# Router logits taken as eight extra columns of two projections, in a pre-LayerNorm linear-attention and mixture-of-experts kernel

## What is computed

```python
scores = jnp.einsum('bhld,bhsd->bhls', Q, K)
out = jnp.einsum('bhls,bhsd->bhld', scores * causal, V)   # then @ wo.T + wo_b
x = x + attention(layernorm(x))
xm = layernorm(x).reshape(-1, 128)
logits = xm @ Wg                     # 128 x 8
probs = softmax(logits); topk_p, topk_i = top_k(probs, 2)
# for each token and each of its 2 experts e, weighted with topk_p:
h = relu(xm @ W1[e] + b1[e]); ye = h @ W2[e] + b2[e]
x = x + weighted sum of the two ye
```

## Time and profile before

| | us |
|---|---|
| median of 3 runs | 308.91 (308.56 to 309.41) |
| the profiled execution | 308.35 |
| its span (first to last instruction) | 306.6 |

### The profile page before, as it was taken

How to read it: one execution, slowest core, us unless ns; L and a number is a source line. 1 busy time by engine, 2 the same in 40 slices (tenths; PEclk the granted TensorE clock), 3 DMA queues, 4 the chain that set the end, 5 groups by cost and what they waited for, 6 DMA issues and landing times.

```text
span 306.6 us, 6357 instructions
## 1 busy us (share of the span) xinstructions
PE 244.9 (80%) x1392; PEld 176.5 (58%) x1392; DVE 195.5 (64%) x584; ACT 174.1 (57%) x701; POOL 179.1 (58%) x175
## 2 busy tenths in 40 slices
PE   0589999999999999987779976969399999896000
PEld 0234566666666666655557865857388778774000
DVE  5938999889998989999652456323143343342184
ACT  3243358888888888777678743445155556552000
POOL 3255492205868686876361777777777676676100
PEclk9999999999999999999566998899689999999655
DMA  7940000000111110111160222234443333211499
GB/s 208 310 145 0 1 2 0 0 4 17 37 37 35 38 36 28 43 36 55 34 169 17 62 74 66 70 84 127 132 116 103 92 89 87 68 47 36 155 356 310
DMA packets 32400, 25.50 MB, mean 83 GB/s; under 512 B 4305, under 2 KB 30169, under 8 KB 32364
## 3 DMA queue, kind: packets, MB, share of 16 engines
q1 hardware_dynamic: 23808, 14.52, 17.6%
q0 software_dynamic: 4320, 8.47, 8.4%
q10 hardware_dynamic: 4236, 2.10, 2.3%
HBM read 13.92 MB, written 11.61 MB: 83 GB/s over the span
## 4 chain that ended last, share of the span: by engine, by line
PE 53%; issue 13%; DVE 10%; DMA 9%; POOL 5%; ACT 4%; SPq 3%; ACTq 1%; POOLq 0%; DVEq 0%
PE ps L870 17%; PE ps L840 8%; PE ps L967 6%; PE ps L956 6%; POOL returned L402 4%; DMA back<-returned 3%; PE ps L879 2%; DMA returned<-y_sb,xt 2%; PE ps L892 2%; PE ps L842 2%; SPq L321 2%; DVE back L623 2%; POOL dispatched L374 2%; DVE o_sb L636 2%; PE ps L861 2%
## 5 line engine op out<-in xcount | busy, mean ns | idle before, releaser
L402 POOL DMA_INDIRECT returned<-y_sb,xt x71 | 70.4, 991 | 34.2 <-issue 20.9
L374 POOL DMA_INDIRECT dispatched<-rows,slot x64 | 64.3, 1005 | 37.8 <-ACT rows L473 21.5
L793 DVE TENSOR_SCALAR y_sb<-ps,xt 128x128 f32<-128x128 f32 x71 | 24.9, 350 | 73.4 <-PE ps L968 72.4
L870 PE MATMUL ps<-back,causal 128*128 128x512 f32 x128 | 62.8, 614 | 0.4 <-DVE back L614 0.4
L967 PE MATMUL ps<-w_sb,hT 128*128 x284 | 52.1, 309 | 6.4 <-DVE y_sb L793 4.8
L956 PE MATMUL ps<-xT,w_of 128*128 128x128 f32 x284 | 50.0, 302 | 2.7 <-ACT hT L546 1.9
L538 ACT ACTIVATE xT<-ps 128x128 f32<-128x128 f32 x71 | 19.6, 276 | 55.6 <-PE ps L949 54.4
L967 PEld LDWEIGHTS ps<-w_sb,hT 128*128 128x128 f32 x284 | 40.1, 204 | 19.0 <-issue 18.8
L358 POOL TENSOR_TENSOR back<-qkv 128x1024 f32<-128x1024 f32 x16 | 31.3, 1955 | 31.4 <-ACT qkv L494 31.1
L546 ACT ACTIVATE hT<-ps,b_col 128x128 f32<-128x128 f32 x142 | 43.9, 364 | 1.7 <-PE ps L956 1.4
L956 PEld LDWEIGHTS ps<-xT,w_of 128*128 128x128 f32 x284 | 40.0, 204 | 5.0 <-issue 4.1
(11 more groups left out here) (142 smaller groups left out, 415.9 us busy)
## 6 DMA issues: line engine op xcount, KB each, us to landing
xt<-dispatched SPq DMA_DIRECT2D x71, 65.0 KB, 2.0
back<-returned SPq DMA_DIRECT2D x8, 512.0 KB, 7.6
x_sb<-x SPq DMA_DIRECT2D x8, 256.0 KB, 5.0
out<-x_sb ACTq DMA_DIRECT2D x8, 256.0 KB, 6.6
returned<-y_sb,xt POOLq DMA_INDIRECT x71, 2.3
w_sb<-w SPq DMA_DIRECT2D x1, 1024.0 KB, 5.9
w_sb<-w SPq DMA_DIRECT2D x2, 512.0 KB, 7.2
dispatched<-rows,slot POOLq DMA_INDIRECT x64, 2.4
```

The lines of the kernel that those rows point to most:

```text
L374: pool.indirect_dma_start(out=dispatched[:, :], out_offset=bass.IndirectOffsetOnAxis(ap=slot[:, g * K + k:g * K + k + 1], axis=0), in_=row ...
L402: pool.indirect_dma_start(out=returned[:, :], out_offset=bass.IndirectOffsetOnAxis(ap=xt[:, n % G, D:D + 1].bitcast(I32), axis=0), in_=y_s ...
L793: dve.tensor_scalar(y_sb[:, n % G, :], ps_y, xt[:, n % G, D + 1:D + 2], None, ALU.mult).then_inc(y_done, 1)
L870: mm = pe.matmul(ps_run[g % 2][:, u, :], causal[:, :], outer[:, g % OUTER_RING, 512 * u:512 * (u + 1)], start=True, stop=True)
```

## The change

The logits are no longer computed from the transposed, normalized second tile. Wg is centred once (each column minus its mean), so that the mean of a token drops out of the product, and it then stands as 8 columns beside the weights of two projections: behind Wq, Wk, Wv (`wqkv_sb` has 392 columns), and behind Wo as Wo times the centred Wg (`wo_sb` has 136), with its part of the bias. ScalarE writes the 8 columns of the first projection, times the first LayerNorm's deviation, beside x in `x_sb` (tiles of 136 columns now); VectorE's residual addition is 136 wide and its last 8 columns are the logits, but for the second reciprocal deviation, with which `softmax_start` multiplies them. The stages `gate`, `transpose2` and `xn2T_out` are gone. Softmax, top two, places and rank run one slot earlier, `chosen` one slot earlier and ahead of `rows_out` in ScalarE's slot, and the dispatches lag 15 slots. The first count is waited for 3 slots earlier, and the first table is built in VectorE's slot 30 and no longer 32. GpSimd makes the outer products of all tiles but 13, 16, 19, 22, 25, 28 and 31, which VectorE makes. The block steps still begin at slot 36.

```diff
-    STATE_AFTER = 7
+    STATE_AFTER = 6
+    DISPATCH = 15
+    FIRST_COUNT = N
+    BLOCKS_FROM = N + 4
+    XE = D + E
...
+    def on_vector(g):
+        return g >= 12 and g % 3 == 1
-            sp.dma_start(wqkv_sb[:, :], w_qkv).then_inc(w_qkv_in, 16)
+            sp.dma_start(wg_sb[:, :], w_gate).then_inc(w_g_in, 16)
+            sp.dma_start(wqkv_sb[:, 0:3 * D], w_qkv).then_inc(w_qkv_in, 16)
...
+            sp.dma_start(bo_col[:, :], b_o.rearrange("(d one) -> d one", one=1)).then_inc(bo_in, 16)
...
@@ GpSimd @@
             def outer_product(g):
-                if g % 2:
+                if on_vector(g):
                     return
...
-            for s in range(N + 16):
-                if s >= 16:
-                    dispatch(s - 16)
+            for s in range(N + DISPATCH):
+                if s >= DISPATCH:
+                    dispatch(s - DISPATCH)
...
@@ ScalarE @@
             def qkv_out(g):
+                wait(act, std_done, 1 + (g >= AHEAD[1].start) + (g >= AHEAD[2].start))
+                act.activation(x_sb[:, g, D:XE], ps_xg, ACT.Identity, scale=std1[:, g:g + 1]).then_inc(xg_done, 1)
                 act.activation(qkv[:, g % QKV_RING, :], ps_qkv, ACT.Identity).then_inc(qkv_done, 1)
...
-            tile_stages = [(10, mean2_out), (12, exponentials), (10, spread2_out), (0, qkv_out), (10, variance_log2), (11, xn2T_out), (10, scale2_out),
-                           (-1, xnT_out), (10, shift2_out), (6, qT_out), (10, rows_out), (-2, normalize), (7, oT_out), (13, chosen),
-                           (-2, deviations_ahead)]
+            tile_stages = [(10, mean2_out), (11, exponentials), (10, spread2_out), (0, qkv_out), (10, variance_log2), (10, scale2_out),
+                           (-1, xnT_out), (10, shift2_out), (6, qT_out), (12, chosen), (10, rows_out), (-2, normalize), (7, oT_out),
+                           (-2, deviations_ahead), (0, gate_weights)]
...
@@ VectorE @@
             def add_residual(g):
                 wait(dve, att_mm, g + 1)
-                dve.tensor_tensor(tile(g), ps_att, tile(g), ALU.add).then_inc(x2_done, 1)
+                wait(dve, xg_done, g + 1)
+                dve.tensor_tensor(x_sb[:, g, :], ps_att, x_sb[:, g, :], ALU.add).then_inc(x2_done, 1)
...
             def softmax_start(g):
-                wait(dve, lg_mm, g + 1)
-                dve.tensor_reduce(gmax[:, :], ps_lg, AX_X, ALU.max).then_inc(gmax_done, 1)
+                wait(dve, rstd2_done, g + 1)
+                wait(dve, x2_done, g + 1)
+                dve.tensor_tensor(lg[:, :, :], x_sb[:, b * T:(b + 1) * T, D:XE],
+                                  norm2[:, b * T:(b + 1) * T, 0].unsqueeze(2).to_broadcast([P, T, E]), ALU.mult).then_inc(lg_done, 1)
+                wait(dve, lg_done, b + 1)
+                dve.tensor_reduce(gmax[:, :], lg[:, :, :], AX_X, ALU.max).then_inc(gmax_done, 1)
...
-            tile_stages = [(5, add_residual), (9, softmax_end), (1, attend_sum), (8, softmax_start), (0, attend), (0, scales_ahead),
-                           (9, places), (2, state_out), (-2, outer_product)]
+            tile_stages = [(5, add_residual), (8, softmax_end), (1, attend_sum), (7, softmax_start), (0, attend), (0, scales_ahead),
+                           (8, places), (2, state_out), (-2, outer_product), (-2, gate_bias_split)]
...
-                if s == N:
+                if s == FIRST_COUNT - 2:
                     first_table()
...
@@ TensorE @@
             def project(g):
-                pe.matmul(ps_qkv, xnT[:, g % RING, :], wqkv_sb[:, :], start=True, stop=False)
+                pe.matmul(ps_qkvg, xnT[:, g % RING, :], wqkv_sb[:, :], start=True, stop=False)
...
+            def gate_weights(g):
+                if g == 1:
+                    pe.transpose(ps_woT, wo_sb[:, 0:D], ident[:, :]).then_inc(woT_mm, 1)
+                elif g == 3:
+                    pe.matmul(ps_wo_gate, woT[:, :], wqkv_sb[:, 3 * D:3 * D + E], start=True, stop=True)
+                    pe.matmul(ps_bo_gate, bo_wide[:, :], wqkv_sb[:, 3 * D:3 * D + E], start=True, stop=True).then_inc(gate_mm, 1)
...
-            tile_stages = [(3, running_sums), (11, gate), (5, q_transposed), (7, o_transposed), (5, sum_state), (-1, project),
-                           (-2, transpose1), (10, transpose2), (7, project_out), (12, rank)]
+            tile_stages = [(3, running_sums), (5, q_transposed), (7, o_transposed), (5, sum_state), (-1, project),
+                           (-2, transpose1), (7, project_out), (11, rank), (0, gate_weights)]
```

More of the change, by code:

```diff
@@ L228, in tile, with outers @@
         def tile(g):
-            return x_sb[:, g * P:(g + 1) * P]
+            return x_sb[:, g, 0:D]
+        def on_vector(g):
+            return g >= 12 and g % 3 == 1
+        def outers(g, vector):
+            return sum(on_vector(i) == vector for i in range(g + 1))
         def states(g):
@@ L916, in rank @@
                 wait(pe, before_done, b + 1)
-                wait(pe, x2_done, g + 5, N)
+                wait(pe, x2_done, g + 4, N)
                 wait(pe, placeof_done, b)
```

152 lines of the change are left out of this document (94 added, 58 removed).

## The result

The changed kernel is slower: a median of 317.05 us (315.72 to 319.17, 4 runs) against 309.16 us (308.56 to 309.71, 4 runs) of the kernel before, a ratio of 1.026 (95% interval 1.020 to 1.033). The forecast of 304.2 us and its range of 300.5 to 309.8 missed it, on the wrong side. The profiled execution took 317.8 us with a span of 316.1, so 9.5 us more of span than before.

What follows compares the result with a forecast made beforehand. TensorE was taken to bound the tile stage, then VectorE its end and GpSimd's chain the blocks. +1.0 - 6.2 + 2.5 - 0.6 - 1.0 - 0.4 = -4.7 us gave 304.2 us, range 300.5 to 309.8.

Steps and rivals of the forecast that it cites:

- part 4: End of tile stage on VectorE: attend of tile 30 to residual of tile 28 keeps its contents despite earlier table; -0.6 us.
- Part 1: First slots: new 8-column activation, transpose of Wo and small products add time, fewer VectorE outer products save some; +1.0 us.
- Part 2: TensorE's slots 10 to 32 without gate and transpose2: 23 slots save 0.27 us each; -6.2 us.
- Part 3: Tile stage: VectorE 98% full, its outer products and GpSimd's operations contend for the shared port; +2.5 us.
- Parts 5 and 6: Slots 37 and 38 lose a transpose and gate product, -1.0 us; blocks 0 and 1 lose a TensorE wait, -0.4 us.
- Part 7: After send-back 1: GpSimd's full chain and all behind it keep their lengths; 0 us.
- The slower rival: Tile stage: VectorE's seven outer products each wait 1.49 us for a GpSimd one, 10.4 us, giving 312.1 us; chance 0.12.
- The signs of being wrong: TensorE idle over 5 us in slots 15 to 33, residual 28 to send-back 1 growing, or TensorE's clock falling earlier.

Runs made afterwards that it cites:

- e1: Changed kernel with VectorE's split of the gate's bias reading its operands from PSUM; stage 107.17 us, ratio 0.984 to the kernel before.
- f2: Changed kernel with GpSimd held until VectorE has split the gate's bias, operands still in SBUF; stage 107.19 us, ratio 0.994 to the kernel before.
- e4: e1 with the outer products divided as before, VectorE odd tiles and GpSimd even; stage 115.53 us, ratio 0.999 to the kernel before.
- g3: Changed kernel with split from PSUM, table and count two slots later, and 18 added VectorE operations; stage 117.02 us, ratio 1.031 to the kernel before.
- h4: h1 with VectorE making the outer products of tiles 12, 15, ... 30; stage 112.49 us, ratio 1.016 to the kernel before.
- k1: Changed kernel with split from PSUM and the count behind TensorE's other work of its slot, table still early; tail 35.9 us, ratio 0.996.
- k2: h1 run again, beside k1 on one chip; median 305.92 us, tail 33.1 us, ratio 0.991 to the kernel before.
- h2: Changed kernel with only the early count moved behind TensorE's other work of its slot; tail 35.9 us, ratio 1.022 to the kernel before.
- f1: Changed kernel run again, unaltered, on another chip; stage 114.88 and 114.98 us, ratio 1.019 to the kernel before.
- h1: Changed kernel with split from PSUM, table and count two slots later, count behind TensorE's other work; median 305.92 us, ratio 0.987 to the kernel before.
- f4: Changed kernel with split from PSUM, table and count two slots later, first transpose of tiles 8 to 31 done twice; stage 107.79 us, ratio 0.983.
- runs e and f: Two groups of experiment runs, on chips where the kernel before took 352 to 356 us; ratios compared only within the same letter.

## Why the prediction was wrong

The span grew by 9.5 us: -0.2 until the first `attend`, +6.8 in the stage, +3.8 in the tail, -0.9 behind. Without the split's waits the stage is 107.2, 1.0 to 1.3 below before (e1, f2). The steps that failed are one that the sum leaves out, the gate's bias split, and one that part 4 put at nothing, the earlier table and count; parts 2 and 3 then gave less than reckoned.

- **Part 1, the start, +1.0:** near for what it names. Tile 0's running sums start at 21.74 instead of 21.05, with the new activation at 0.27 us and not 0.2; by the first `attend` the difference is gone (23.70 and 23.86). It had one more meeting: the copy of Wo's bias to `bo_wide` (L763, 128 x 128, one input in SBUF) took 1.61 us there, and 0.24 in e4, where GpSimd pauses; e4's sums start at 21.58, so it cost 0.2 us at most.
- **A step that the sum does not have.** The gate's bias split stands in VectorE's slot 2 and nowhere in the sum. Its cost stands there as nothing, and it is 7.8 us (e1, f2), 5.9 in waits and some 2 that TensorE's clock would account for. This alone turns a forecast of faster into slower.
- **Part 2, TensorE's slots, -6.2:** as far as tile 28 that is 18 x 0.27 = -4.9. TensorE did get free, 2.92 us in 8 slots, but the stage without its excess fell only from 106.8 to 103.9 us, by 2.9. The prediction saw VectorE at 98% and let TensorE's saving through whole; slots of 3.7 to 3.85 us never came (4.02).
- **Part 3, contention, +2.5:** the size was near. That the new division is needed holds (e4 is worse without it), and the excess besides the split is 3.3 us where it was 1.5. What failed is the list of who can meet: only the seven large products were in it. Half of the excess is `lg`, and in g3 and h4 it is `shifted`, both small. GpSimd's first dispatch came at 73.37, since all of the routing was late by the split; in e1 it came at 65.68, as worked out. Parts 2 and 3 together gave -3.7; the stage of the mended kernels gives -1.0 to -1.3.
- **Part 4, VectorE's end, -0.6:** the stretch from `attend` of tile 30 to the residual of tile 28 fell from 11.40 to 10.64, as said. The step that failed is "Only the softmax's start and the wait for the count leave it, to an earlier slot". The wait for the count is one of TensorE's as well, with the running sums of tile 29 behind it (2.04 us, then 1.54 for VectorE and the lower clock), and the table ahead of tile 31's `attend` delays it and the residuals behind. Forecast 0, measured +2.8 for the table (k1 against k2) and +1.2 to 1.4 for the count's place (h2; the second figure is a difference of tails between two chips, and the kernel before differs by 1.3 between two chips as well).
- **Parts 5 and 6, -1.4:** not seen in the changed kernel; with table and count moved back the tail is 33.1 us for 33.5 and 34.8 of before. From the residual of tile 28 to send-back 1 it is 19.15 us where it was 19.06. What was taken away did not shorten the row of residuals: that of tile 31 follows 11.3 us behind that of tile 28, and followed 7.95 before.
- **Part 7, 0:** right, 38.49 us between send-backs 1 and 15 for the 38.7.
- **The slower rival** had the right mechanism and the wrong place and price: 10.4 us on seven products, which lost 1.8 in the stage, and nothing on four operations of 8 columns, which lost 5.9.
- **The signs of being wrong:** TensorE idles for 6.5 us between slots 15 and 33, over the 5 that were set (from 70.07 to 148.23 us; 1.05 before). The time from the residual of tile 28 to send-back 1 did not grow. The clock fell later and not earlier, a mean of 1.00 between 145 and 155 us (0.54 before), but it then stayed at 0.50 until 175, where it was 0.67 and 0.77 before.

The prediction cites the Trainium skill's page "SBUF — State Buffer" for the exclusive lock. The same section, "SBUF: two separate sides", says that the lock is taken by VectorE's operations in a two-port mode as well as by those with two SBUF inputs, and holds "for the whole instruction". The page's section "Who interferes with whom" names copies and casts among those that can enter such a mode. The traces agree for both: a cast with one SBUF input took 1.82 us, a subtraction with two 1.87, and reading PSUM they took 0.16 and 0.17. It sets no size below which an operation would be exempt, and the prediction had read the rule as one about large products.

## What to carry to other kernels

Where one engine waits for the whole of another's operation, count small operations like large ones: the price is what is left of the other's, 0.4 to 2.5 us here, whatever the size of one's own. Take the operand from PSUM, or place the operation where the other engine pauses. A saving on the busiest engine can come through only in part when the next one is at 95% and the two wait for each other; here 2.9 of the 4.9 us reckoned did. And a wait that is moved forward is to be followed on each engine that carries it, with all that is queued behind.

## What the runs showed of the hardware

- Four VectorE operations of 8 columns or less took 1.82, 1.87, 1.88 and 0.94 us, each ending within 0.03 us of a GpSimd operation's end. They are four of a chain of six beside a row of GpSimd operations without a gap; the same operations took 0.16 and 0.17 us when GpSimd stood still (f2) or when they read PSUM (e1).
- The wait goes the other way too. A dispatch transfer of GpSimd that begins 0.08 us or more behind the start of an outer product of VectorE, and before its end, ends 0.8 to 0.9 us behind the product's end (95.35 behind 94.51 in the changed kernel, 106.55 behind 105.72 before), and so lasts up to 1.97 us in place of 0.96. The first dispatch of a trace, where it does, ends 1.05 behind.
- VectorE's operations with a PSUM operand never waited so: all 24 rows of `state` are 0.27 to 0.29 us in each of the traces, next to the same GpSimd work, and no row with a PSUM operand lasts 0.2 us more than the shortest of its form in any trace.
- Which operations meet repeats from run to run and chip to chip (95.77 and 107.34 us in the first trace, 96.20 and 107.77 in f1), so a phase shift of one tile was worth up to 9 us (h1, h4), and that is no noise.
- TensorE fell to its lower clock (1.2 of 2.4 GHz) behind an idle of 4.74 us and behind one of 2.04: four running sums then took 3.24 and 2.90 us in place of 1.93.
- A matmul's row is longer than what it adds: 0.27 us against 0.11 from start to start (f4).
- Chips differ: on those of the runs e and f every kernel took some 40 us longer, 33 of them behind send-back 0. The cause was not looked for.
